# One core, a two-expert mixture, attention, and the mixture again: the hand-written order of 3132 steps is written anew

## The reference, cut to what matters

```python
x = L0_attn_x                                       # 8 x 512 x 256, float32
x = x + 0.5 * ffn(layernorm(x), gate_w, w1, w2, w3)
x = x + attn(layernorm(x), W_q, W_k, gain, bias, log_mix, log_scale)
x = x + 0.5 * ffn(layernorm(x), gate_w, w1, w2, w3)

def ffn(x, gate_w, w1, w2, w3):                     # 8 experts, d_ff 512
    probs = softmax(x @ gate_w.T)
    weights, idx = top_k(probs, 2)                  # 2 experts of each token
    weights = weights / weights.sum(-1)
    out = (silu(x @ w1[e].T) * (x @ w3[e].T)) @ w2[e].T   # for e in idx
    return sum over the two of weights * out

def attn(x, ...):                                   # per batch of 512 tokens
    A = the 8 earlier tokens s with the largest x[t] . x[s]
    score = (x W_q)(x W_k)^T / sqrt(32), -1e9 outside A
    msg = softmax(score) @ x
    blended = mix * x + (1 - mix) * msg
    return gelu(blended * gain + bias) * scale
```

## Time and profile before

| | |
|---|---|
| median of 3 runs | 826.82 us (823.93 to 833.67) |
| the profiled execution's own time | 827.08 us |
| its span | 825.2 us |
| PE busy | 703.2 us (85%) |
| VectorE, ScalarE, GpSimd busy | 556.6, 507.1, 455.9 us |
| mean granted TensorE clock over the span | 0.945 |
| DMA | 149.44 MB, 181 GB/s |

### The profile page before, as it was taken

One profiled execution on the slowest core, in us unless ns is written; L12 is line 12 of the kernel. 1 busy time (PEld: TensorE's weight loads), 2 busy tenths in 40 slices (PEclk: granted clock), 3 DMA queues, 4 the chain that ended last, 5 costly groups with the idle time before them and its releaser, 6 DMA issues.

```text
span 825.2 us, 17489 instructions
## 1 busy us (share of the span) xinstructions
PE 703.2 (85%) x4672; PEld 431.8 (52%) x4672; DVE 556.6 (67%) x1596; ACT 507.1 (61%) x980; POOL 455.9 (55%) x545
## 2 busy tenths in 40 slices
...
GB/s 341 427 182 92 89 228 185 161 136 143 172 180 116 167 155 152 206 153 195 176 152 177 150 176 151 152 178 181 148 128 180 182 189 149 134 154 211 257 256 285
DMA packets 313270, 149.44 MB, mean 181 GB/s; under 512 B 293789, under 2 KB 297245, under 8 KB 312413
## 3 DMA queue, kind: packets, MB, share of 16 engines
...
q0 software_dynamic: 17888, 37.65, 15.7%
...
## 4 chain that ended last, share of the span: by engine, by line
PE 38%; DMA 13%; SPq 10%; DVE 9%; ACT 6%; issue 5%; POOL 2%; POOLq 0%; ACTq 0%; DVEq 0%
PE B L1224 23%; PE B L1236 11%; DMA t_ht<-hs 3%; SPq L1094 3%; DMA hs<-t_s,t_POS 3%; DVE t_X L1738 2%; SPq L1056 2%; SPq L1041 2%; DMA t_gh<-t_gp 1%; DMA t_ph<-t_p 1%; DMA t_s<-yt 1%; SPq L1117 1%; DVE t_gp L1729 1%; PE B L1288 1%; PE B L1249 1%
## 5 line engine op out<-in xcount | busy, mean ns | idle before, releaser
L1224 PE MATMUL B<-t_W,t_ht 128*128 x1704 | 401.5, 386 | 26.2 <-DMA t_ht<-hs 14.2
L1224 PEld LDWEIGHTS B<-t_W,t_ht 128*128 128x128 f16 x1704 | 167.3, 99 | 208.3 <-issue 44.4
L1723 DVE SCALAR_TENSOR_TENSOR t_th<-B,t_K,t_th 128x512 f32<-128x512 f32 x142 | 105.9, 748 | 112.7 <-PE B L1224 103.8
L998 POOL DMA_INDIRECT yt<-t_W,t_idx x107 | 110.9, 1036 | 118.3 <-ACT t_W L1373 83.3
L1236 PE MATMUL B<-t_W,t_gh 128*128 x1284 | 159.7, 276 | 17.4 <-DMA t_gh<-t_gp 8.3
L951 POOL DMA_INDIRECT hs<-t_s,t_POS x112 | 120.3, 1074 | 68.9 <-issue 29.9
L1236 PEld LDWEIGHTS B<-t_W,t_gh 128*128 128x128 f16 x1284 | 124.6, 99 | 53.2 <-issue 24.2
L1357 ACT ACTIVATE t_th<-B,t_K 128x512 f32<-128x512 f32 x142 | 96.6, 682 | 78.5 <-PE B L1224 77.0
L1366 ACT ACTIVATE t_gp<-t_th 128x512 f16<-128x512 f32 x107 | 66.4, 623 | 50.8 <-DVE t_th L1723 46.6
L990 POOL DMA_DIRECT2D t_idx<-hs x142 | 80.4, 572 | 30.6 <-DMA yt<-t_W,t_idx 9.6
L1729 DVE TENSOR_TENSOR t_gp<-t_th,t_gp 128x512 f16<-128x512 f32 x107 | 74.5, 702 | 19.5 <-ACT t_gp L1366 18.5
...
## 6 DMA issues: line engine op xcount, KB each, us to landing
t_W<-wk SPq DMA_DIRECT2D x6, 2048.0 KB, 25.2
...
t_ht<-hs SPq DMA_TRANSPOSE x142
t_idx<-hs POOLq DMA_DIRECT2D x142, 0.5 KB, 2.7
```

The source lines that it names most:

```text
L998: eng.indirect_dma_start(yt_d[L], bass.IndirectOffsetOnAxis(ap=IDX[:, n % RING:n % RING + 1], axis=0), YO[n % YR], None).then_inc(d_y[n % ...
L1224: t = eng.matmul(B[b][:], HT[n % HTR][:, (2 * hl + db) * 128:(2 * hl + db) * 128 + 128], W16[:, bass.ds(expert[n] * 4096 + (db * 2048 + wl ...
L1723: eng.scalar_tensor_tensor(out=th[:], in0=B[b1][:], scalar=K[:, 7:8], in1=th[:], op0=ALU.mult, op1=ALU.mult).then_inc(free[b1], 1)
```

## The change

The string ORDER is replaced by another of the same 3132 steps. The order within a stream of steps is unchanged, what is interleaved with what differs. Its first and last lines:

```diff
 ORDER = (
-    "))Bt)%)Bt))feY%fezYBY(KLK$tYL$KLKL$$)))B)t%f+++++qe%xwYfepv!Y++KL+K$YYD-+L$!s+++KLKBt%^fe^!!!!V))B++++z=$tYYK=^?"
...
-    "FEFE*Fg1J****UUUUJgJg1Jg1gUUUUggg")
+    "))Bt)%)Btz%feYY))B(KfeYY)))LK$L$)BttKLKL$$%f+eqxw+%+p++fY+Kv!YsLD!e-K++$++++YYBt%L$KLKL>f^eV$!!^!!))B+t+$++qxzYY"
...
+    "UUUUEF*EF*EEJFFJg**JggUUUUggg")
```

With it go a few edits of waits. The counter of the spare rows' writes becomes one for each layer, three waits count another, equally placed step, and the plan lets plo come only after factors:

```diff
-        yield Want("plo", (b, i), gives=(("sm", b, i),))
+        yield Want("plo", (b, i), (("factors", ()),), gives=(("sm", b, i),))
...
-        d_spare = sem("d_spare")
+        d_spare = [sem(f"d_spare{i}") for i in range(2)]
...
-                    e.wait_ge(d_spare, 2 * 112)
+                    e.wait_ge(d_spare[0], 112)
+                    e.wait_ge(d_spare[1], 112)
...
-                        e.wait_ge(d_spare, 112 * (L + 1))
+                        e.wait_ge(d_spare[L], 112)
...
-                    e.wait_ge(s_rstd, nth("aggr", n))
+                    e.wait_ge(s_rstd, nth("root", n))
...
-                        e.wait_ge(s_hh, 4 * nth("normal", n) - 3)
+                        e.wait_ge(s_hh, 4 * nth("nhi", n) - 3)
...
-                    e.wait_ge(s_ac, nth("qk", b, m))
+                    e.wait_ge(s_ac, nth("qkout", b, m))
```

More of the change, by code:

```diff
@@ new lines @@
+    "=?==KLKw^%p^+$!!)??fe)BLYY=vt_=+$KLK$L$%??q==?fx?e=!^=!!!!ws^!)?)?+puWuWYKB=+^_t=Y?v!+LKL=%++?=??=?=?!1!1=$$+?Wu"
+    "W^1zfeYY^KLKL;$$;.=qxwN!1!1>;;ps1.^^S>vD-~~~!!N_~~P=?=WW?;;W[=?=!1S^1.y2?=??==N>;;P?^S}}V!!1^.N!!1!1>;.^P;>;;.^?"
+    "_|!1|!N>}}h}}}h}N}SPQSEh;;>F.~|~PW;.WQSPQNEF;SPN>;;!!!|_QhQQ_uE>FE.~~~FNSSP*E*F_}WW~uW;;~*Q>;EW}}*.NS~~.cPFQ;>NP"
+    "S;*~~~~.*aWuQWPE;>F*NSP~~~~~;EQF;>.;;>NS.NE;};>WFSPPE;_W}QQ.FNRS.y;>EFN;;E>.NSPP**_*~QW~F;**WH~WQEQkF;.SEFXuWWPN"
+    "SPQQQ>;;>.W;E;>NWF.ESFNPQ~~****;EF;.NSSPPQW>;E;QF>;.yNSPE.;NFE>SPQQF~*_;~_***EF*;uWu>E;WW.FE.FNSP;NSQ~~~>~P~*;.;"
@@ new lines @@
+    ">NSP;*;.N>;E~~SF*JJUUU;U))B_W.~t>;QQEF~W*Nu.;%NPSPfeYYJWJWQT>;;.NUEF*>;;E.S>;_USPPUWTU))BQWWQF.;WutNsI%mon&moNnS"
+    "/f>P;;>;<#.Z.&NGi~~/<jQM#Wl;E&FZSSG>E;#bN/PQWQ<_iFZ*~SeP&jGEYl#;>F.Y_/iTT<b1dCE;Pd;Nb.jZGCmon*~m_NAQ>;lioFdnj&#;"
+    "S>b.CA/<ZP*SPGAQulWW&E/<#dCZiF*j~~A&Wl/NG;EQ;>&Or*SFE;i.)j;F<#)NB**bdtESPZ%b.Nf>;e/;<F>.;CYPYNJJ#QQWlWQS.~~**~~~"
+    "~SGEFbi;d>AZ;UU;NSGPuE:$>;*UFjQl:bUW.iE_))PBt*Fd;>EPj.%~*Nf;;$>eFCS.lWWNdYCA1A*YPTTQQWyq;;NCx>mownmoSP.nEF&QAuWp"
+    ";;SO/#&>N;v#.EP;>/.*<!NZr<FGiZ))jN^E&SGS;PFPB;~~QWWSEQ#~l.>;;/&#>!!^!QN<ZPQWWijlF.Sb1Ed;N/t_G<Z%Fb1iPG*E*F.~fJWJ"
@@ L157 @@
+    "SPFFEQWF;;W*~>E;***.NSP.;>N;;S.QWJJUUPNUUJQS>;P;>;..;>NNSFJPW;;EyUUUUSPFJW.W>;;>.;NQS.;~~~NJUUUUJJUuWWQQPS>uEEFF"
+    ";;>NUPQEUUJJU*FS**.N*QEFQSWEWW;.;>UPFEg2g1QWUFNSEPUJJPQ***;.;NS>;;.NSEFP**PUQQQ>;;>;.NUFSP*;.NSPUUygEQEQF*F*JJg1"
+    "UUUUEF*EF*EEJFFJg**JggUUUUggg")
 class Plan:
```

46 lines of the change are left out of this document (17 added, 29 removed).

## The result

Measured beside each other on one chip, the changed kernel took 823.24 us (median of 22 runs, 817.26 to 832.63) and the kernel before 827.27 (22 runs, 820.23 to 834.82). The ratio is 0.9955, with a 95% interval from 0.9934 to 0.9976: faster by 0.2 to 0.7%. 0.0045 x 827.27 is 3.7 us (the medians differ by 4.0), half of the 7.4 us forecast. (A ratio leaves disturbed runs out, so it can differ a little from that of two medians.)

What follows compares the result with a forecast made beforehand. TensorE was taken as the bound from 144 to 800 us, with GpSimd closer to it before. Terms -3.5 - 3.8 - 1.0 + 2.4 - 1.5 = -7.4 us from 827.08 gave 819.7 us; range 808 to 833, likeliest case 815 to 824.

Steps and rivals of the forecast that it cites:

- place 1: Group 1's positions: GpSimd's first write at 55.9 us, not 59.47; -3.5 us, between nothing and -4.3.
- the 48 writes and their 79.6 us stay as they are: GpSimd's writes of groups 1 to 3 keep their length, 59.47 to 139.06 us before, if nothing new makes GpSimd wait.
- Rival (c): First part gains nothing: group 3's positions 3 to 10 us late for GpSimd, total up to 827; chance 0.24 shared with (d).
- Place 2: Tile 109's load issued directly behind load(108): TensorE's 3.07 us hole and its clock fall go; -3.8 us, between 0 and -4.8.
- no hole and no clock below 1.00 between tiles 105 and 112: Sign that moving tile 109's load works: TensorE has neither a hole nor a lowered clock in that stretch.
- Block 3's last transpose: Attention block 3: TensorE's 1.85 us wait for the last probabilities transpose goes; -1.0 us, between -1.85 and 0.
- The allowance for new holes: Middle, 144 to 800 us: the new order makes some holes of its own; +2.4 us, between -10 and +15.
- TensorE's time not busy below 30 us: Sign for the middle: from tile 9 to 800 us TensorE is not busy for less than 30 us.
- place 3: The tail: last gate transposes go ahead of the final blocks' fetches, shortening TensorE's waits; -1.5 us, between 0 and -3.9.
- (a): The middle gives more: half of the holes in 144 to 800 us go, -16 us, total 806; chance 0.2 (below 815).
- (b): Attention matmuls moved earlier make TensorE wait on SyncE's transposes: +20 us, total 839; chance 0.12 (above 832).
- (d): Nothing measurable: gains at the three places are refilled in the middle, 824 to 830; chance 0.24 shared with Rival (c).

Runs made afterwards that it cites:

- k18: The changed kernel, unaltered, measured a fourth time beside the kernel before: 817.29 us, ratio 0.9891.
- k1: The kernel before with only the change's edits of waits, its order kept: 820.52 us, ratio 0.9971.
- k3: Order of before until tile 9, the changed order until tile 133's first matmuls, then before again: 822.69 us, ratio 1.0000.
- k4: Order of before until tile 133's first matmuls, then the changed order: 822.39 us, ratio 0.9979.
- k13: The kernel before once more, measured beside the kernel before: 826.66 us, ratio 1.0010.
- k15: The kernel before with TensorE's register load which(0) moved from behind score(5,1) to ahead of sum(12): 828.90 us, ratio 1.0010.
- k9: The changed kernel, unaltered, measured a third time beside the kernel before: 822.77 us, ratio 0.9962.
- k11: The changed kernel with six TensorE steps moved to mend holes, score(18,0) among them: 822.79 us, ratio 0.9967 to the kernel before.
- k14: The changed kernel with TensorE's register load which(0) moved back behind score(5,1): 824.58 us, ratio 0.9977 to the kernel before.
- k6: Changed order until tile 9, then order of before with only load(109) moved to behind load(108): 814.16 us, ratio 0.9881.
- k5: The changed kernel, unaltered, measured a second time beside the kernel before: 814.71 us, ratio 0.9900.
- k16: The changed kernel with TensorE's sum(12) to sum(15) put ahead of score(3,0) and score(3,1): 817.29 us, ratio 0.9898 to the kernel before.
- k2: Changed order until tile 9's first matmuls, then the order of before: 816.98 us, ratio 0.9881.
- k7: Changed order until tile 9, order of before until tile 133's first matmuls, then changed order again: 815.19 us, ratio 0.9922.
- k10: Changed order only until GpSimd's first write of group 1, then the order of before: 830.58 us, ratio 1.0046.
- k12: Changed order until GpSimd's first write of group 2, then the order of before: 828.84 us, ratio 1.0031.
- k8: The changed kernel with TensorE's score(18,0) moved behind up(59,1): 811.51 us, ratio 0.9870 to the kernel before.
- k17: The changed kernel with sum(12) to sum(15) ahead of the scores and score(18,0) behind up(59,1): 812.09 us, ratio 0.9853 to the kernel before.

## Why the forecast was right and wrong, step by step

**Where the long stretch starts (place 1, -3.5).** This is the step that failed in the recorded result. The forecast let scale(1) and router 1 run as soon as TensorE's rows end and so put group 1's first write at 55.9 and tile 9 at 141. VectorE had the results 5 and 8 us after those rows, the write came at 63.38 and tile 9 at 147.69: 3.3 us later than before instead of 3.5 earlier.

The mechanism was right where nothing stalled. The write that the mark waits for landed at 49.4 (forecast 50.2), and group 1's first write came at 56.02 in k18 (forecast 55.9), at 56.5 on average of the eight profiles without the stall, against 59.4 of the four with the old start: -2.9. ScalarE's and GpSimd's timelines of k18:

```profile
49.38 0.20 ACT L1351 ACTIVATE t_s<-t_ids 128x2 int32<-128x2 int32 x1 [0.71 <-DMA hs<-t_s,t_POS]
49.49 2.06 ACT L1323 ACTIVATE t_hp<-t_X,t_ve 128x256 f32<-128x256 f32 x4
```

```profile
56.02 1.89 POOL L952 DMA_INDIRECT hs<-t_s,t_POS  x1 [0.76 <-DVE t_POS L1658]
...
129.91 0.96 POOL L952 DMA_INDIRECT hs<-t_s,t_POS  x1 [0.30 <-issue]
130.87 0.59 POOL L970 DMA_DIRECT2D hs<-t_ph  x1
...
```

The step "the 48 writes and their 79.6 us stay as they are" failed as well: they took 130.87 - 56.02 = 74.9 us, since each issue was shorter. (Half of that lies in before's own profile: the other profiles with the old start, k1, k3, k4, k13 and k15, have 77.1 to 77.8.) So tile 9 came at 137.7 on average of eight profiles, against 142.9 of the four with the old start (before, k1, k3, k4): -5.2, beyond my bound of -4.3. With the stall it came at 146.6 on average (changed, k9, k11, k14) against 143.2 (k13, k15): +3.3, beyond the other bound, nothing.

Rival (c) did not happen: with the mark ahead of normal(7), GpSimd met group 3's first write at 98 to 100 us without the 3 to 10 us wait; only with the stall was there one, of 2.3 us in the changed kernel's profile and 1.5 in k9.

**The middle (places 2 and 3's block, -2.4 in sum).** Place 2 was right in mechanism, as k6 shows, and the hole at tile 109 went in every profile with the new middle. But another came back 11 us on, ahead of down(105). The timelines of SyncE and TensorE and a stretch, changed kernel:

```profile
664.87 1.65 SPq L1058 DMA_TRANSPOSE t_ht<-hs  x1
...
668.12 1.25 SPq L1096 DMA_TRANSPOSE t_gh<-t_gp  x1
...
672.36 2.36 PE L1238 MATMUL B<-t_W,t_gh 128*128 x12 [2.12 <-DMA t_gh<-t_gp]
...
670.00:678.00 8.00, 5.88 (x28) 0.79 1.07 217
```

TensorE waits there for a gate transpose, issued behind the next load, and the clock falls behind it. The forecast looked for the returning hole at tile 112 and at a load; its sign "no hole and no clock below 1.00 between tiles 105 and 112" failed. All ten profiles with the new middle have a wait of 0.8 to 2.2 us there, ahead of down(105) or down(106), and k3 and k5 one more of 1.2 and 2.6 us for an eviction. (k6, with load(109) alone moved, waits 0.8 us for a load ahead of tile 112.) From tile 100 to tile 113 the new order (k3, k5, k16, k18) takes 55.8 us on average and the old (before, k1, k2, k4, k7) 56.7, and the new one has a down block less in that stretch, 1.3 us of work. So without the stall these profiles show nothing of the 3.8 us at tile 113.

Block 3's last transpose: no profile of the new middle waits for it, but msg(1,3) now waits up to 2.6 us for another. The forecast's 1.85 us was one execution's, for k2 and k6 do not wait there in the old order either. The allowance for new holes, +2.4, was too small. Without the stall, tile 9 to tile 133 took 615.6 us on average in the new order (k3, k5, k16, k18) and 614.9 in the old one (before, k1, k4, k2, k7): +0.7 in place of -2.4. The two cuts are not quite the same. In the changed order 127 down blocks stand ahead of tile 133 and in the old one (and in k3) 128, so 1.3 us of work is counted with the tail. Tile 9 to the last join holds the same work in both and takes 675.2 us on average in the old order (before, k1, k2) and 674.1 in the new (k5, k16, k18): the middle and the tail together gave -1.1 in place of -3.9. "TensorE's time not busy below 30 us" failed too: the idle times over 0.2 us from tile 9 to tile 141 sum to 31.3 before, 34.6 in the changed kernel, 34.0 in k5 and 33.1 in k18.

In the sets with the stall the middle did pay: 613.8 us on average (changed, k9, k14) against 618.3 (k10, k12, k13, k15), -4.5. Nearly all of it lies between tiles 100 and 113, around the place of load(109): 60.6 to 62.0 us in the old order, 54.7 to 57.3 in the new, of which 1.3 are the down block that it has less there. TensorE's timeline of k13, the kernel before, ahead of tile 109:

```profile
648.35 2.24 PE L1236 MATMUL B<-t_W,t_gh 128*128 x19
...
653.72 0.27 PE L1236 MATMUL B<-t_W,t_gh 128*128 x1 [1.18 <-issue]
655.13 0.27 PE L1236 MATMUL B<-t_W,t_gh 128*128 x1 [1.15 <-issue]
656.07 2.74 PE L1236 MATMUL B<-t_W,t_gh 128*128 x12 [0.67 <-ACT t_W L1373]
```

A down block starts its matmuls singly, 0.7 to 1.5 us apart, with nothing in the profile that it waits for ("issue"). In k10, k12 and k15 one wait of 3.4 to 4.3 us, put down to an eviction, stands in that place, ahead of down(102). The 1.93 to 3.07 us wait ahead of tile 109 is hidden behind this longer one.

**The tail (place 3, -1.5).** Right in mechanism, and in size as far as the profiles tell. Ahead of the last four down blocks all nine profiles with the old end wait 2.8 to 5.1 us and all eleven with the new one 0.5 to 2.7 (forecast: under 2.5). From tile 133 to the last join the old end took 59.9 us on average without the stall (before, k1, k2, k6) and the new one 58.0 (k4, k5, k7, k8, k16 to k18): -1.9. k3, which has the old end as well, took 56.7; with it the old end is 59.2 and the gain 1.3. Part of what went came back earlier: the new end has a wait of 0.7 to 1.7 us for a gate transpose ahead of a down block some 10 us before (1.68 us, at 792.77, in the changed kernel). In that profile one wait, for an eviction, is left ahead of the last four down blocks, and none for a gate transpose:

```profile
800.83 4.09 PE L1238 MATMUL B<-t_W,t_gh 128*128 x36
804.76 1.47 PE L1238 MATMUL B<-t_W 128*128 x12
806.18 1.50 PE L1238 MATMUL B<-t_W,t_gh 128*128 x12
808.58 1.50 PE L1238 MATMUL B<-t_W,t_gh 128*128 x12 [0.91 <-ACT t_yo L1375]
```

**The edits of waits (nothing).** k1 can't be told from before.

**The sum.** Without the stall: -5.2 + 0.7 - 1.9 = -6.4 us by the profiles, -7.7 and -8.1 by the medians (k5, k18). With it: +3.3 - 4.5 - 0.6 = -1.8 by the profiles (the tail 59.1 to 58.5), -4.0 and -3.8 by the medians (recorded, k9). The forecast's -7.4 is the first; what was measured first was the second. That the total agreed with one of them owes something to luck: place 1 was forecast too small by 1.7 and the middle's gain too large by 3.1. Rivals (a) and (b) did not come: holes went and came in equal sum. (d) came closest in the recorded result, but with gains at two places that were refilled by the stall, not by the middle.

k17 beats both kernels: 812.09 us beside 825.38 of before and 817.29 of the changed kernel in its set.
